# Second attention: one more stage in the pipeline of a head, with probabilities in three buffers

## The reference

```python
q = (xn @ Wq + bq).reshape(B, S, H, dk).transpose(0, 2, 1, 3)   # H = 8 heads, dk = 32
k = (xn @ Wk + bk).reshape(B, S, H, dk).transpose(0, 2, 1, 3)
v = (xn @ Wv + bv).reshape(B, S, H, D).transpose(0, 2, 1, 3)
scores = jnp.einsum('bhsd,bhtd->bhst', q, k) / jnp.sqrt(dk)
p = jax.nn.softmax(scores, axis=-1)
att = jnp.einsum('bhst,bhtd->bhsd', p, v)
out = att.reshape(S, B, D, H).sum(axis=-1).reshape(B, S, D)
```

## Time and profile before

| | us |
|---|---|
| median of three runs | 2752.63 |
| lowest, highest run | 2743.34, 2756.63 |
| the profiled execution, its own time | 2752.09 |
| its span in the profile | 2750.3 |
| of it TensorE matmuls busy | 2431.2 (88%) |
| weight loads busy | 2034.0 (74%) |
| DVE busy | 1921.9 (70%) |
| ACT busy | 1155.6 (42%) |
| GpSimd busy | 419.4 (15%) |

### The profile page before, as it was taken

The page is one execution under the profiler, slowest core; times in us unless marked ns, Lnnn a source line. Parts: engine busy times, 40 slices in busy tenths (PEclk is TensorE's granted clock), DMA queues, the critical chain, the costliest instruction groups (busy, mean ns, idle before and its releaser), DMA issues. The chain is left out here.

```text
span 2750.3 us, 119322 instructions
## 1 busy us (share of the span) xinstructions
PE 2431.2 (88%) x50848; PEld 2034.0 (74%) x50848; DVE 1921.9 (70%) x7392; ACT 1155.6 (42%) x3690; POOL 419.4 (15%) x412
## 2 busy tenths in 40 slices
PE   1678999999999999987858858999999999999999
PEld 0455677777777777654536648999999999999998
DVE  4567877777777777788666646767767776766664
ACT  3124555555555555556336723333333333333333
POOL 0000000000000000000009911222222222222222
PEclk9678999999999999999759958999999999999999
DMA  5000000000000000010013330000000000000000
GB/s 169 1 2 3 5 5 5 5 5 5 5 5 5 5 5 5 6 42 27 4 43 89 93 93 22 9 9 9 9 9 9 9 9 9 9 9 9 5 5 6
DMA packets 52747, 53.66 MB, mean 20 GB/s; under 512 B 24934, under 2 KB 46840, under 8 KB 50042
## 3 DMA queue, kind: packets, MB, share of 16 engines
q1 hardware_dynamic: 46868, 26.81, 3.6%
q0 software_dynamic: 2000, 14.68, 1.6%
q10 hardware_dynamic: 3350, 4.54, 0.5%
HBM read 39.46 MB, written 6.55 MB: 17 GB/s over the span
## 5 line engine op out<-in xcount | busy, mean ns | idle before, releaser
L105 PE MATMUL p<-xn,m_h 128*128 128x128 f16 x6144 | 557.5, 219 | 0.0
L105 PE MATMUL p<-xn,m_l 128*128 128x128 f16 x3072 | 528.8, 219 | 0.0
L105 PEld LDWEIGHTS p<-xn,m_h 128*128 128x128 f16 x6144 | 479.9, 98 | 1.8
L2047 POOL TENSOR_TENSOR xn<-qkv_w,xn 128x384 f16<-128x384 f32 x256 | 233.9, 914 | 908.6 <-ACT xn L2005 908.6
L576 PE MATMUL lg_b<-xn,lh 128*32 128x256 f16 x6144 | 297.8, 289 | 79.4 <-DVE lh L1016 77.8
L992 DVE STREAM_TRANSPOSE gt<-lg_b 128x512 f32<-128x512 f32 x324 | 230.2, 710 | 188.0 <-PE lg_b L576 187.5
L814 ACT ACTIVATE gl<-gt 128x128 f32<-128x128 f32 x324 | 100.3, 309 | 601.9 <-DVE gt L992 601.4
L829 ACT ACTIVATE hm<-xy,b 128x512 f32<-128x512 f32 x512 | 348.0, 680 | 0.1
L105 PEld LDWEIGHTS p<-xn,m_l 128*128 128x128 f16 x3072 | 300.6, 98 | 0.7
L1931 PE MATMUL po<-m_h,xn 128*128 128x256 f16 x1536 | 292.6, 272 | 1.9 <-DVE xn L2086 1.9
L576 PEld LDWEIGHTS lg_b<-xn,lh 128*32 128x32 f16 x6144 | 158.5, 101 | 164.1 <-DVE lh L1016 129.3
(11 more groups left out here) (385 smaller groups left out, 6218.9 us busy)
## 6 DMA issues: line engine op xcount, KB each, us to landing
m_stage<-in_m_w POOLq DMA_DIRECT2D x12, 1024.0 KB, 6.0
hs<-in_m_w SPq DMA_DIRECT2D x14, 384.0 KB, 3.2
xs<-in_x POOLq DMA_DIRECT2D x1, 2048.0 KB, 8.4
x_dram<-x SPq DMA_DIRECT2D x16, 128.0 KB, 2.1
xs<-in_l_wv SPq DMA_DIRECT2D x1, 2048.0 KB
attention_dram<-att SPq DMA_DIRECT2D x16, 128.0 KB, 2.9
xn<-x_dram SPq DMA_DIRECT2D x16, 128.0 KB, 2.5
out_dram<-xn SPq DMA_DIRECT2D x16, 128.0 KB, 2.2
```

What stands on the lines that cost most here:

```text
L105: ins = pe.matmul(out, w[wp](k), x[xp](k), start=start, stop=last and k == KT - 1 and xp == 1, skip_group_check=True)
L2047: pool.tensor_tensor(a_l[:, n % 2, :], a32[:, n % 2, :], a_h[:, n % 2, :], ALU.subtract).then_inc(a_lo, 1)
```

## The change

The loops of the three engines get one step more. `prob` has three buffers. The exponentials of head g wait for the turn of head g−3. ACT takes the high half of head g−2 in step g, DVE the low half of head g−3, TensorE the values of head g−3. `finish` moves from h = 1 to h = 2, which in an even step stands ahead of the row maximum. The buffers of `pt`, `pt_h` and `pt_l` and the waits of `turn`, `high` and `values` are as before.

```diff
-        prob = sb("prob", [P, 2, TT, BT])
+        prob = sb("prob", [P, 3, TT, BT])
...
-                        last = pe.matmul(pt[g % 2][:, u, s_ * P:(s_ + 1) * P], prob[:, g % 2, s_, u * P:(u + 1) * P],
+                        last = pe.matmul(pt[g % 2][:, u, s_ * P:(s_ + 1) * P], prob[:, g % 3, s_, u * P:(u + 1) * P],
...
-            for g in range(GH + 2):
+            for g in range(GH + 3):
                 b, h = g // NH, g % NH
                 if 1 <= g <= GH:
                     turn(g - 1)
                 if g % 2 == 0 and g // 2 + 1 < GH // 2:
                     scores(g // 2 + 1)
-                if g >= 2:
-                    values(g - 2)
+                if g >= 3:
+                    values(g - 3)
...
                 act.wait_ge(neg_max, g + 1)
-                if g >= 2:
-                    act.wait_ge(t_pe, g - 1)
+                if g >= 3:
+                    act.wait_ge(t_pe, g - 2)
...
-                    act.activation(prob[:, g % 2, s_, :], sc[g % 4][:, s_, :], ACT.Exp, bias=nmax[:, g % 4, s_:s_ + 1],
+                    act.activation(prob[:, g % 3, s_, :], sc[g % 4][:, s_, :], ACT.Exp, bias=nmax[:, g % 4, s_:s_ + 1],
...
-            for g in range(GH + 1):
+            for g in range(GH + 2):
                 b, h = g // NH, g % NH
                 if g < GH:
                     exps(g)
-                if g >= 1:
-                    high(g - 1)
+                if g >= 2:
+                    high(g - 2)
...
-            for g in range(GH + 2):
+            for g in range(GH + 3):
                 b, h = g // NH, g % NH
-                if 2 <= g:
-                    low(g - 2)
+                if 3 <= g:
+                    low(g - 3)
                 if g % 2 == 1 and g + 2 < GH:
                     row_max(g + 2)
                 if h == 0 and b > 0:
                     inverse(b - 1)
                     if b < B:
                         projected(b, 2)
-                elif h == 1 and b > 0:
+                elif h == 2 and b > 0:
                     finish(b - 1)
```

## The result

The changed kernel took 2765.78 us (median of eight runs, 2763.02 to 2771.04) against 2743.76 us for the kernel before (eight runs, 2741.85 to 2756.63): a ratio of 1.0066 with a 95% interval of 1.0049 to 1.0083. It is slower. The ratio is estimated over all runs; the medians alone lie 22.0 us apart (a quotient of 1.0080), because five of the eight runs before took 2742 to 2744 us and three, the profiled one among them, took 2752 to 2757. The forecast was a ratio of 2769.5 / 2752.1 = 1.0063.

A forecast was written before the change was run, and what follows sets the result against it. Waits, with no engine full, were taken to bound the second attention stage. From 2752.1 us, 5.8 + 6.4 + 0.5 = +12.7 us without the clock and +4.7 us for the clock gave 2769.5 us; range 2757 to 2782 us.

The forecast's parts named there:

- What bounds the stage: Second attention stage: no engine is full, waits hold it, and ACT, with 50.0 us of waits, is not on the path.
- The ring: Even-odd step pairs: low half, turn, scores, maximum wait in a circle; +0.83 us at h = 6, seven times, 5.8 us.
- h = 0 at nothing: Pair of steps starting at head 0: 4.25 us before, no time added by the change.
- The division in h = 2, +1.06: Division moved between low half and maximum at h = 2, delaying what queues behind: +1.06 us, six times, 6.4 us.
- h = 4 at nothing: Pair of steps starting at head 4: 4.72 us before, no time added by the change.
- High halves: "worth nothing by itself": ACT taking high halves two heads back: its waits for the turn shrink, but no time is gained by this alone.
- The clock, +4.7: TensorE clock drops while batches are projected: nine instead of six, three more at 1.58 us each, +4.7 us.
- The ends, +0.5: Last batch, which projects nothing, and the drain with one more step: +0.5 us.
- The first: Rival: waits for value products and the six clock drops vanish, nothing takes their place; 2726.6 us, chance 0.06.
- second: Rival: the added stage is inert, waits only change names; 2752 us, chance 0.10.
- third: Rival: h = 6 pairs lose 5.8 us, but the h = 2 division is hidden or drops go; 2758.4 us, chance 0.18.
- The fourth: Rival: the clock drops at every wait for q_l and k_l; 2777.4 us, chance 0.16.

The follow-up runs named there:

- the first experiment: Kernel before with only the low halves and value products one step later, high halves and the two buffers of prob as before: 2766.59 us, ratio 1.0084.

## Why the prediction was right, and where it was not

- *What bounds the stage.* Right. ACT's 50.0 us of waits were not on the path: the third buffer alone left the batch at 17.56 us.
- *The ring, +0.83 in each h = 6 pair.* Right in place and nearly in size: 4.04 instead of 3.94, so +0.93, seven times 6.5 us. The turn waits for L1583, as forecast, and moving the scores ahead takes the loss of this pair away. The missing 0.1 us is the time from a low half to a turn, 0.82 to 0.83 us (DVE 1532.48 to turn 1533.31), where I had used 0.74, that to a value product.
- *h = 0 at nothing.* 4.39 for 4.25: +0.14, the same 0.1 us.
- *The division in h = 2, +1.06.* Right: 6.53 against 5.48 in the undisturbed batch of the first experiment. h = 4 at nothing: right, 4.71.
- *High halves: "worth nothing by itself".* Wrong as a statement about the part alone. It cost 0.5% by ACT's queue. It holds only in company with the later low halves.
- *The clock, +4.7.* The direction was right, places and price were wrong. I expected nine drops, six at q_l and three at k_l. There were eight: one in each of the seven q_l stretches, none at k_l, where three had been, and one early in the first batch, ahead of its h = 2 turn. In the six batches from division to division there were six, before five. Above the undisturbed 19.67 us (6.53 + 4.71 + 4.04 + 4.39) these six batches hold 6.5 us; before, above 17.56, they held 7.9. So a drop cost about 1.1 us there and not 1.58, and the clock took 1.4 us less, since part of each half-clock stretch now fell into idle time: of the one that began at 1532.68, the first 0.63 us passed before the turn at 1533.31.
- *The ends, +0.5.* Mis-sized. From the first row maximum to the last division the stage took 156.73 us before and 174.36 after, +17.6. The six batches hold 11.2 of it. The remaining 6.4 lie in the first batch, which had two clock drops instead of one, and in the last, where the run of small float32 matmuls for the next part took 8.8 us (1593.44 to 1602.20) instead of 6.9 (1579.40 to 1586.27), with the clock at half all through it. Less about one for the h = 6 and h = 0 pairs that lie there, that is 5.3 us against 0.5. Most of it is the clock again, and no cost of the drain: by my estimate 1.6 us for the added drop of the first batch (its h = 2 stretch took 7.15 us, before 5.48) and 1.9 for the matmuls, of which only the second part had been at half clock before.

Terms of the sum against measured, in us: ring and division 12.2 and 13.8 (6.5 + 1.0 + 6.3), clock +4.7 and −1.4 in the six batches, ends +0.5 and about +5.3. Sorted by cause, with the clock's 3.5 us moved out of the ends, it is 12.2 and 13.8, clock 4.7 and about 2.1, ends 0.5 and about 1.8. The ring and the division were understood; that the sum, 17.4 against 17.6 in the stage, is better than its parts is luck, since the errors cancelled.

*The rivals.* The first (waits go, nothing takes their place) fell with the 31.1 us ahead of the turns; its deciding condition, low halves done before TensorE reaches the turn, is never met at the odd turns. The second and third fell with the h = 6 stretch and the division at 1.85. The fourth fell with the k_l stretches, in which no drop began. The Trainium skill's rule on independent matmul groups that rotate through PSUM banks (Perfetto Trace Analysis, Matmuls), weighed in the prediction, does not cover this case: two banks rotate and the turns wait 31.1 us all the same. The Trainium skill's remark that regular bubbles can mean too few buffers (Perfetto Trace Analysis, Optimization Strategy) fits here at most for the buffer that the waits name: the third one for `prob` changed nothing.

A third PSUM buffer for the turned probabilities might open the ring as well. It was not tried: by the code the stage already holds eight PSUM tensors of 2 KB per partition, and a ninth would have meant another layout.

## What to carry to other kernels

When a pipeline gets one more stage, list for each buffer between two stages how many items now live in it: here `prob` got the third buffer, while the turned probabilities, whose readers moved back too, kept two, and that closed a ring. On engines with a fixed order of instructions, look at what stands directly behind the instruction that now waits; issuing an independent producer (the scores) ahead of the waiting turn was worth some 15 us here, and nothing in the kernel before, whose turns did not wait for low halves. And before deepening anything, find the operation that ends the longest stretch: two low parts taken 0.60 us earlier took 1.2 us off each batch, while the restructuring as made added 2.1.

## What was not expected of the hardware

Drops of TensorE's clock locked on to the period of a batch. In the changed kernel and in the one with late high halves each of the six batches from division to division had exactly one, always in the q_l stretch, and the latter's six batches were 20.43 to 20.46 us long. The same holds for the changed kernel with the division behind the maximum and with early q and k. In all four the drops of the six batches begin 20.48 us apart, and in the changed kernel the batches themselves come down to that spacing, 20.85, 20.71, 20.60, 20.54 and 20.51 us, before the last (21.28). Whether the batch sets the spacing or the spacing the batch is not shown, but mending 0.6 us of waiting inside such a stretch gave nothing back. In the kernel before with early q and k no drop came in six batches at 16.36 us. For the division's edit, and for q_l in the changed kernel, the clock and not the wait decided what was gained.

The stage did not begin at the same time in every profile, though no kernel changes anything ahead of it: the first row maximum stood at 1431.7 us in one and at 1447.6 us in another. The spread between runs of one kernel is of this size, so stage and batch lengths tell more here than single times.
